# Constant bf16 products between the score and weight matmuls of an attention loop

## What is computed

```
x = layernorm(x + attention_1(x))
x = layernorm(x + ffn_block(x))

def ffn_block(x):                     # 16 heads of width 16
    h = layernorm(x, ln1_g, ln1_b)
    q, k, v = h @ Wq, h @ Wk, h @ Wv
    attn = softmax(q @ k.T / sqrt(16))        # no mask
    x = x + (attn @ v) @ Wo
    m = layernorm(x, ln2_g, ln2_b)
    probs = softmax(m @ Wg)                   # 8 experts, the best 2 of each row
    return x + sum over the 2 of wt * (gelu(m @ W1[e] + b1[e]) @ W2[e] + b2[e])
```

## Time and profile before

| | us |
|---|---|
| median of three runs | 2608.37 |
| the profiled execution, its own time | 2620.64 |
| span of the profiled execution (first to last instruction) | 2618.9 |
| slots 0 to 551 of the second attention (1320.10 to 2007.90) | 687.8 |

### The profile page before, as it was taken

The page is one execution under the profiler, slowest core; times in us unless marked ns, Lnnn a source line. Parts: engine busy times, 40 slices in busy tenths (PEclk is TensorE's granted clock), DMA queues, the critical chain, the costliest instruction groups (busy, mean ns, idle before and its releaser), DMA issues. The chain is left out here.

```text
span 2618.9 us, 38830 instructions
## 1 busy us (share of the span) xinstructions
PE 2207.4 (84%) x12343; PEld 1169.6 (45%) x12344; DVE 1690.7 (65%) x3493; ACT 1369.2 (52%) x2634; POOL 922.6 (35%) x766
## 2 busy tenths in 40 slices
PE   4589898989999999999468899889888279999991
PEld 2244444444444444444222223223223268888881
DVE  4577878786878778676156655666662545555556
ACT  1366566766666665766225665656656223333332
POOL 4463645554463736433411211221111123333330
PEclk9677687877778786777778988788877689999996
DMA  1210111111121201110141122424524641111116
GB/s 47 66 54 20 57 41 49 49 48 38 37 61 26 62 23 57 33 33 9 39 58 33 26 58 50 113 90 110 133 81 138 261 158 48 47 45 45 48 41 200
DMA packets 140066, 172.35 MB, mean 66 GB/s; under 512 B 23873, under 2 KB 120338, under 8 KB 137874
## 3 DMA queue, kind: packets, MB, share of 16 engines
q1 hardware_dynamic: 131426, 149.58, 20.3%
q0 software_dynamic: 7488, 20.46, 2.6%
q10 hardware_dynamic: 1008, 0.54, 0.1%
HBM read 105.47 MB, written 65.01 MB: 65 GB/s over the span
## 5 line engine op out<-in xcount | busy, mean ns | idle before, releaser
L1243 DVE TENSOR_REDUCE NM<-sP 128x1 f32<-128x512 f32 x512 | 332.6, 684 | 233.4 <-PE sP L1126 231.8
L401 POOL TENSOR_TENSOR YZ<-XL 128x1280 f32<-128x1280 f32 x128 | 297.7, 2326 | 433.2 <-DVE XL L687 400.9
L1058 ACT ACTIVATE PT<-tP 128x512 f32<-128x512 f32 x512 | 285.6, 604 | 260.4 <-PE tP L1138 258.6
L476 ACT ACTIVATE YZ<-YZ,gsc 128x512 f32<-128x512 f32 (+3 forms) x512 | 321.9, 655 | 143.9 <-DVE YZ L663 143.6
L674 DVE CUSTOM_DVE_ANT_0 YZ<-SeP,YZ 128x512 f32<-128x512 f32 (+3 forms) x512 | 244.0, 487 | 228.7 <-PE SeP L541 187.1
L460 ACT ACTIVATE XL<-mP 128x512 f32<-128x512 f32 (+1 forms) x384 | 201.2, 525 | 181.3 <-PE mP L551 180.5
L566 PE MATMUL tPa<-ident,YZ 128*128 128x128 f32 x1280 | 281.4, 346 | 0.3
L1489 ACT ACTIVATE H<-hP,B1T 128x256 f32<-128x256 f32 x312 | 131.0, 471 | 264.5 <-PE hP L1568 264.4
L468 ACT ACTIVATE PTa<-tPa 128x512 f32<-128x512 f32 (+1 forms) x384 | 202.9, 529 | 91.3 <-PE tPa L572 86.9
L540 PE MATMUL SeP<-STG 48*128 48x512 f16 (+3 forms) x512 | 185.0, 361 | 59.4 <-DVE mn L674 58.5
L663 DVE SCALAR_TENSOR_TENSOR YZ<-YZ,XL 128x1280 f32<-128x1280 f32 x128 | 210.5, 1644 | 5.5 <-POOL YZ L401 5.1
(11 more groups left out here) (301 smaller groups left out, 4112.1 us busy)
## 6 DMA issues: line engine op xcount, KB each, us to landing
STG<-planes_a_scratch SPq DMA_DIRECT2D x512, 32.0 KB, 1.9
X<-in_L_ffn_W SPq DMA_DIRECT2D x32, 512.0 KB, 4.2
weight_planes<-X SPq DMA_DIRECT2D x64, 256.0 KB, 2.5
STGb<-planes_scratch SPq DMA_DIRECT2D x96, 128.0 KB, 7.0
planes_a_scratch<-HI SPq DMA_DIRECT2D x64, 128.0 KB, 1.7
planes_a_scratch<-LO SPq DMA_DIRECT2D x64, 128.0 KB, 1.8
STG<-planes_a_scratch SPq DMA_DIRECT2D x128, 64.0 KB, 2.1
Y<-results_scratch SPq DMA_DIRECT2D x16, 512.0 KB, 8.8
```

What stands on the lines that cost most here:

```text
L401: pool.tensor_tensor(YZ[:, h % NYZ, :], XL[:, h % NXL, :], XL[:, h % NXL, :], ALU.mult).then_inc(y_ready, 1)
L476: act.activation(w, w, ACT.Square, bias=gsc[:, b % 2, 1, i, hh:hh + 1], scale=gsc[:, b % 2, 0, i, hh:hh + 1]).then_inc(hyp_ready, 1)
L1058: act.activation(PT[:, p % 4, par, kt, :], tP[x % 3][:, :], ACT.Exp).then_inc(exp_done, 1)
L1243: dve.tensor_reduce(NM[:, g % 2, col:col + 1], sP[n % 2][:, :], AX.X, ALU.max, negate=True).then_inc(max_done, 1)
```

## The change

After the work of each slot from 0 to 551, PE adds matmuls of the constant identity matrix (bf16, 128 rows) with itself repeated four times (512 columns). They go into the projection bank that holds no live use, `bank[used % 2]`, and nobody reads them. Their number comes from a count of columns: `columns(n)` adds up what the slot already streams (fp32 work is weighted by its passes), and as many matmuls of 512 columns follow as fit below `KEEP` = 2100. The first of them in a slot waits for `bank_out`, until ACT has emptied that bank's last use. They are called fillers below.

```diff
@@ -801,6 +801,7 @@
             SHIFT = 256.0
+            KEEP = 2100
             RT = NT // 2
@@ -1108,6 +1109,21 @@
+                    def columns(n):
+
+                        total = T * (0 <= n < TILES) + T * (0 <= n - LAG < TILES)
+                        for kt in range(NT):
+                            if at_group(n, 7, 2 * kt) is not None:
+                                total += 4 * T
+                        if at_group(n, 8, 2) is not None:
+                            total += NT * 2 * P
+                        for kind, i, step, t in USES:
+                            if at_batch(n, step, t) is not None:
+                                total += {"q": 4 * CH * T, "v": 8 * CH * C, "w": 8 * CH * C, "l": 4 * CH * NT * E}.get(kind, NT * 2 * P)
+                        return total
+
+                    used = 0
@@ -1173,6 +1189,7 @@
                             u = nth[kind, i, b]
+                            used = u + 1
@@ -1208,6 +1225,12 @@
                             mm.then_inc(bank_full, 1)
+                        if 0 <= n < TILES + LAG and used < len(nth):
+                            for f in range((KEEP - columns(n)) // T):
+                                if f == 0:
+                                    pe.wait_ge(bank_out, used - 1)
+                                pe.matmul(bank[used % 2][:, :], identb[:, :], identb[:, :].unsqueeze(1).broadcast_to([P, NT, P]),
+                                          start=True, stop=True)
```

## The result

The changed kernel takes 2724.6 us, median of four runs (2716.4 to 2744.2), where the kernel before took 2608.0 beside it: a ratio of 1.045 with a 95% interval from 1.040 to 1.050. It is slower, as forecast, and inside the range; the forecast of 2700 was 25 us too low. The profiled execution took 2716.4 us of its own with a span of 2714.6.

The account below looks back on a forecast made before the run. PE was taken to bound the second attention (the stage): 535 us own work, 159 filler columns and 58 shape changes make 752, plus 15 waits and 12 clock: 779, 91 above 687.8. Forecast 2700 us, range 2655 to 2765.

Parts of the forecast that it names:

- Light slot: Slot of the second attention without products with values: with two fillers 1.06 us, where it took 0.60 to 0.9 before.
- the rival in which the clock is worth more than the slots: Fillers fall wholly into PE's waits in the second attention: stage 656 us, kernel 2576 us; chance 0.06.
- Changes of shape: On PE, between 128-row fillers and neighbours of 48 or 50 rows: 613 more switches at 0.095 us, 58 us.
- The rival in which they are free: Switching between fillers and neighbouring matmuls on PE costs nothing: stage 694 to 721 us, kernel 2614 to 2641; chance 0.07.
- Columns: Streaming of the fillers on PE: 738 of 512 columns at 0.216 us each, 159 us.
- Sharing: Fillers stand between slots whose matmuls ran together on PE's array; no term, since PE's bound counts every matmul alone.
- the 535 us: PE's own work in the second attention before the change, at 2.4 GHz throughout, with every matmul alone.
- Waits: PE's remaining idle time in the second attention: 11 us for split maxima, 4 for others; 15 taken, bounds 0 and 49.
- Clock: Time lost to PE's low clock in the second attention: 24 us left at half speed, so 12 us lost.
- Head: First 40 slots of the second attention: 36 x 1.05 us plus four projections, 46 us, where they took 35.7.
- The sum: Second attention, slots 0 to 551: 752 us of PE work, 15 idle, 12 lost to low clock: 779, against 687.8 before.
- The rival in which fillers don't hold the clock: PE's clock in the second attention stays at 0.90 (kernel 2771 us) or 0.82 (2850 us); chance 0.12.

## Why the prediction was right, and where it was off

- **Light slot.** 1.06 forecast, 1.07 measured, in the same pieces (0.22, 0.31, 0.22, 0.31). This carries most of the result, and it ends the rival in which the clock is worth more than the slots: that needed 0.79.
- **Changes of shape.** They cost 0.09 to 0.1 both into a filler (0.31) and out of it (0.31), as the earlier trace rows had it. The rival in which they are free falls. The Trainium skill, "TensorEngine Tiling (Array Packing)", section "Key Properties", has the rule that fits: changing the tiling mode drains the engine, and changing the tile does not. By that rule the trace agrees: 0.31 at a change from 50 rows to 128, 0.22 from 48 to 50.
- **Columns.** Taken at 0.216, measured 0.215 to 0.226 between two fillers, mostly 0.226: for the 396 that follow another filler some 4 us.
- **Sharing.** It needed no term, because the 535 us had every matmul alone, and that was right; the pair of 1.54 us is the 2.60 of now.
- **Waits.** 15 forecast, 16 of idle time measured, in the named places: split maxima 5.9 (I had 11), exponentials, the turned result. The one for maxima is gone and the bank costs nothing.
- **Clock.** 12 forecast, about 20 measured. The step that failed in part is that a full budget leaves nothing to fall over. `columns` counts the gate logits as 256 columns, and the chip spends 1.8 us on them in matmuls of 8; behind three of the six sets a fall follows. And I took a wait of a few us on ACT as a wait alone, where it also brings the clock down.
- **Head.** 46 forecast for 40 slots, 49.7 measured.
- **The sum.** 752 and 16 and 20 and 4 are 792, of 797.2 measured; I had 779. The 5 that remain I can't name. So 18 of the 25 us of error lie in the stage. The other 7 have another source: the stages differ by 109.4, the medians by 116.7, and each is set against one execution with its own first attention, 15.5 us slower in the one of before.
- **The rival in which fillers don't hold the clock** did not come, at 0.97. It had its 0.12 for good reason, though: lighter fillers than these come out at 0.90 (fewer of them), 0.88 (48 rows) and 0.78 (128 columns).

That the edit loses is shown from both sides of it: with fewer columns in a filler, fewer fillers or more fillers it stays slower, and it comes back to the kernel before only when fillers share the array with live work and stay out of the slots that did so before.

## What to carry to other kernels

Work that only holds the clock is free only in time that the engine would have idled; price it in the slot with the least slack (its columns, a change of shape on either side, the sharing that it forbids) and compare that with the pace of the engine next to it before you ask what the clock gives. If such work is wanted, give it the shape of its neighbours and another part of the array, and leave alone the places where live matmuls already share. And see first whether the clock's gain can arrive: in the slots where the weight pieces load beside it, it didn't.

## What the runs showed of the hardware

- A low clock can outlast its cause by far: behind one wait of 1.5 us (in the kernel with short fillers) it stayed at 1.2 GHz for over 50 us, with PE busy throughout, when the fillers had 128 columns; with 512 columns it was back in 3.4 to 6.8. Why short matmuls keep it low I did not settle.
- It also fell with no idle time just ahead of it, behind sixteen matmuls of 8 columns: behind three sets of the six, 0.5, 1.4 and 1.7 us after the last of the sixteen had made way.
- Half-height fillers (48 rows) in place of full ones, equal in number and columns, left the clock at 0.88 instead of 0.97. Some of them ran beside another matmul, so this may be their rows or the time that they no longer fill; the runs don't part the two.
- A filler of 48 rows and a live matmul on the other rows started 0.01 us apart, against the order in which the program issues them, and each took 0.39, as it does alone.
